# Attention rows of edgeless nodes made beside the gathers of the attention stages, in a fused GNN kernel

## The reference, cut to what matters

```python
def gat_layer(xf, src, dst, W, a_src, a_dst, b, heads, out_ch):
    n = xf.shape[0]
    h = (xf @ W).reshape(n, heads, out_ch)
    e_src = jnp.einsum('nhc,hc->nh', h, a_src)
    e_dst = jnp.einsum('nhc,hc->nh', h, a_dst)
    e = jax.nn.leaky_relu(e_src[src] + e_dst[dst], NEG_SLOPE)
    ...
    out = jax.ops.segment_sum(alpha[:, :, None] * h[src], dst, num_segments=n)
    return out.reshape(n, heads * out_ch) + b
```

## Time and profile before

| | |
|---|---|
| three runs, median (lowest to highest) | 6930.43 us (6916.66 to 6943.3) |
| profiled execution, span | 6960.0 us; no other time of that execution is given |
| TensorE busy | 70% of the span |
| VectorE, ScalarE, GpSimd busy | 55%, 43%, 51% |
| mean granted clock of TensorE | 0.824 |
| plain stage | about 75 to 1963 us |
| stages 8 to 11 | start at about 4717, 5257, 5800 and 6343 us |

### The profile page before, as it was taken

How to read it: one execution, slowest core, us unless ns; L and a number is a source line. 1 busy time by engine, 2 the same in 40 slices (tenths; PEclk the granted TensorE clock), 3 DMA queues, 4 the chain that set the end, 5 groups by cost and what they waited for, 6 DMA issues and landing times. The chain is left out here.

```text
span 6960.0 us, 128354 instructions
## 1 busy us (share of the span) xinstructions
PE 4844.2 (70%) x28287; PEld 3887.0 (56%) x28362; DVE 3822.9 (55%) x13753; ACT 2996.7 (43%) x7457; POOL 3526.6 (51%) x4581
## 2 busy tenths in 40 slices
PE   4888888888889888997798986660381282183087
PEld 3666666666666676666687876650271172073076
DVE  5666666666644586336676767660361261162076
ACT  3666666666633333444566655550130031031043
POOL 2344434444455274706474747106556556656666
PEclk9999999999989856998899987775695596597555
DMA  3555444454444375536633434322232232133233
GB/s 86 150 162 163 166 169 164 162 172 167 166 119 108 110 200 147 144 95 189 194 110 86 115 90 129 87 78 55 54 102 64 48 103 69 42 102 76 46 106 92
DMA packets 1002699, 815.64 MB, mean 117 GB/s; under 512 B 103821, under 2 KB 836819, under 8 KB 1002617
## 3 DMA queue, kind: packets, MB, share of 16 engines
q1 hardware_dynamic: 908536, 650.27, 30.6%
q0 software_dynamic: 94080, 164.48, 9.8%
HBM read 359.28 MB, written 459.01 MB: 118 GB/s over the span
## 5 line engine op out<-in xcount | busy, mean ns | idle before, releaser
L864 POOL DMA_INDIRECT G<-table,idx_all x1568 | 1519.3, 969 | 1308.5 <-issue 661.4
L1436 PE MATMUL PS<-CR,LO 1*128 1x128 f32 (+3 forms) x4312 | 1069.9, 334 | 273.1 <-ACT CR L1763 272.6
L1436 PE MATMUL PS<-G,S 128*128 (+2 forms) x4312 | 995.7, 318 | 41.3 <-DVE OWN L1304 15.6
L1436 PEld LDWEIGHTS PS<-CR,LO 1*128 1x128 f32 (+1 forms) x4312 | 766.1, 221 | 419.7 <-ACT CR L1763 329.8
L1436 PEld LDWEIGHTS PS<-G,S 128*128 128x128 f32 x4312 | 791.2, 223 | 129.8 <-issue 100.5
L1763 ACT ACTIVATE CR<-PS 65x128 f32<-65x128 f32 (+2 forms) x1274 | 340.8, 268 | 1019.0 <-PE PS L1436 1006.7
L864 POOL DMA_INDIRECT G<-table,idx_l x588 | 568.5, 967 | 398.6 <-DMA table<-RO 220.2
L1433 PE MATMUL PS<-ident,ES 128*98 128x128 f32 x16 | 4.2, 420 | 1003.5 <-DVE ES L476 1003.5
L1433 PEld LDWEIGHTS PS<-ident,ES 128*98 128x98 f32 x16 | 2.6, 191 | 1004.7 <-issue 1004.6
L476 DVE COPY ES<-G 128x392 f32<-128x392 f32 x4 | 2.1, 527 | 1017.1 <-DMA G<-table,idx_all 1017.1
L1436 PE MATMUL PS<-G,FS 128*65 (+2 forms) x2646 | 448.5, 314 | 98.8 <-DVE den L1368 44.4
(11 more groups left out here) (291 smaller groups left out, 11312.6 us busy)
## 6 DMA issues: line engine op xcount, KB each, us to landing
table<-G SPq DMA_DIRECT2D x392, 260.0 KB, 2.7
table<-G SPq DMA_DIRECT2D x392, 256.0 KB, 2.6
table<-RO SPq DMA_DIRECT2D x245, 256.0 KB
table<-RO SPq DMA_DIRECT2D x196, 260.0 KB
OWN<-table SPq DMA_DIRECT2D x196, 260.0 KB
XIN<-xrows SPq DMA_DIRECT2D x196, 256.0 KB
OWN<-table SPq DMA_DIRECT2D x147, 256.0 KB
xrows<-RB SPq DMA_DIRECT2D x147, 256.0 KB
```

Source lines behind the costliest of these rows:

```text
L864: g.indirect_dma_start(G[:, t, 0:w], None, TAB[s], bass.IndirectOffsetOnAxis(ap=idx[:, t:t + 1], axis=0)).then_inc(gat[t % 4].sem, 16)
L1436: return nc.tensor.matmul(o, l, r, start=start, stop=stop)
```

## The change

- The plain stage stores one attention table (8) instead of four, and instead of the output it stores the residual rows x3 into a new table `x_plain`. The products, ReLUs, copies and sums of layers 9 to 11 and of the output go from it. All four hand-written orders are new, and the transposes of the edge attributes use another PSUM bank.
- A new function `beside_gathers(s)` runs on SP, TensorE, ScalarE and VectorE at the start of each attention stage, beside GpSimd's gathers. For stages 8, 9 and 10 (kind "F") it goes over all 98 quads: load the rows of table s, four transposes, ReLU with the bias, four products with the next weights, copy, store into table s + 1. For stage 11 (kind "FO") it loads the rows of table 11 and of `x_plain`, adds both and the bias, and stores the output.
- It works in two sets of buffers (b = 0, 1), lent from S and LO, UT and OT, OWN and RO, GN and U.
- GpSimd waits for the stored rows before the next stage's gathers.

```diff
+        F_IN = [t[:, :, :].rearrange("p s c -> p (s c)")[:, 0:4 * GW].rearrange("p (j c) -> p j c", j=4)
+                for t in (S, LO)]
+        F_HT = [UT, OT]
+        F_OUT = [OWN, RO]
+        F_X = [t[:, :].rearrange("p (j c) -> p j c", j=4) for t in (UT, OT)]
+        F_SUM = [GN, U]
...
+        BESIDE = ["F", "F", "F", "FO"]
...
@@ SP @@
             def plain(m, b):
                 q0, q1, q2, q3 = (earlier((m, 0, b), k) for k in range(4))
+                load_x(q0)
+                keep(q1, "t1", q_a[1], "g", PG[1])
+                keep(q3, "x3", q_v[2], "xc", PX[3])
+                keep(q2, "t3", q_a[2], "g", PG[2])
                 keep_x_norm(q3)
-                load_x(q0)
-                keep(q3, "out", q_v[3], "xf", PY)
-                keep(q3, "t3", q_a[2], "g", PG[2])
+                keep_x(q0)
+                next_attributes(q1)
+                keep(q1, "t2", q_a[1], "t1", PR[2])
+                keep(q2, "t4", q_a[2], "rA", PR[4])
+                keep_attributes(q2)
                 keep(q3, "t8", q_v[3], "r8", PR[8])
-                keep_x(q0)
-                keep(q1, "t1", q_a[1], "g", PG[1])
-                keep(q3, "t11", q_v[3], "r11", PR[11])
-                keep(q2, "t4", q_a[2], "rA", PR[4])
-                next_attributes(q1)
-                keep(q3, "t9", q_v[3], "r9", PR[9])
-                keep(q1, "t2", q_a[1], "t1", PR[2])
-                keep(q3, "t10", q_v[3], "r10", PR[10])
-                keep_attributes(q2)
...
+            def beside_gathers(s):
...
+                def load(m, b):
+                    if not isinstance(m, int) or m:
+                        sp.wait_ge(*((f_t.sem, f_t.at(ph, m * 2 + (b - 2), "turn")) if kind == "F" else
+                                     (f_v.sem, f_v.at(ph, m * 2 + (b - 2), "sum"))))
+                    sp.dma_start(F_IN[b], plain_rows(TAB[s], at(m, b) + EP)).then_inc(f_in[b].sem, 16)
+                    if kind == "FO":
+                        sp.dma_start(F_X[b], plain_rows(XP, at(m, b))).then_inc(f_x[b].sem, 16)
+
+                def store(m, b):
...
+                    sp.wait_ge(f_v.sem, f_v.at(ph, m * 2 + b, "rows" if kind == "F" else "sum"))
...
+                def turn(m):
+                    for b in (0, 1):
+                        store(m, b)
+                        if not isinstance(m, int) or m < last:
+                            load(m + 1, b)
+
+                for b in (0, 1):
+                    load(0, b)
+                turn(0)
+                with sp.Fori(1, last - 1) as m:
+                    turn(m)
...
@@ VectorE @@
+                inverse(q3, 3)
+                shift(q3, 3)
                 x_inverse(q1)
                 x_shift(q1)
+                with_bias(q1)
                 stats(q0, 1)
                 aggregate(q0, 1)
+                hidden(q1)
+                inverse(q0, 1)
+                shift(q0, 1)
+                x_stats(q0)
+                convolved(q1)
                 sampled(q2)
+                stats(q1, 2)
                 residual(q2)
+                aggregate(q1, 2)
                 constant(q2)
+                x_aggr(q0)
+                inverse(q1, 2)
+                shift(q1, 2)
                 stats(q2, 3)
                 aggregate(q2, 3)
+                rows(q3, 8)
...
+                def rows(m, b):
+                    dve.wait_ge(f_r.sem, f_r.at(ph, m * 2 + b, "rows"))
+                    free(m, b)
+                    v.tensor_copy(F_OUT[b][:, :, :], pair(2 + 2 * b)).then_inc(f_v.sem, 1)
...
+                def turn(m):
+                    for b in (0, 1):
+                        if kind == "F":
+                            rows(m, b)
+                        else:
+                            bias(m, b)
+                            total(m, b)
...
@@ TensorE @@
+                turned(q1, 1)
+                turned(q2, 2)
                 hidden(q1, 0)
                 hidden(q1, 1)
+                sampled(q2)
+                attributes(q2)
+                convolved(q1)
+                rows_b(q2)
                 rows_a(q2)
+                turned(q3, 3)
+                rows(q3)
...
+                def turned(m, b):
+                    pe.wait_ge(f_in[b].sem, f_in[b].at(ph, m, "rows"))
+                    for j in range(4):
+                        i = turn(PS[:, b, P * j:P * j + P], F_IN[b][:, j, 0:D])
+                    i.then_inc(f_t.sem, 1)
+
+                def rows(m, b):
+                    pe.wait_ge(f_a.sem, f_a.at(ph, m * 2 + b, "hT"))
+                    if not isinstance(m, int) or m:
+                        pe.wait_ge(f_v.sem, f_v.at(ph, m * 2 + (b - 2), "rows"))
+                    rows4(pair(2 + 2 * b), F_HT[b], WX[:, ph + 1, 0:GW]).then_inc(f_r.sem, 1)
+
+                def two(m):
+                    turned(m, 1)
+                    rows(m, 0)
+                    if not isinstance(m, int) or m < last:
+                        turned(m + 1, 0)
+                    rows(m, 1)
+
+                turned(0, 0)
+                two(0)
+                with pe.Fori(1, last) as m:
+                    two(m)
+                two(last)
...
@@ ScalarE @@
+                turned(q1, 1)
+                turned(q2, 2)
+                hidden(q1)
                 sampled(q2)
+                norm(q3, 3)
+                root(q0, 1)
+                x_norm(q1)
                 attributes(q2)
+                convolved(q1)
+                norm(q0, 1)
+                turned(q3, 3)
+                rows_a(q2)
+                root(q1, 2)
+                x_root(q0)
+                norm(q1, 2)
                 root(q2, 3)
...
+                def turned(m, b):
+                    act.wait_ge(f_t.sem, f_t.at(ph, m * 2 + b, "turn"))
+                    f(F_HT[b][:, :], PS[:, b, :], ACT.Relu, bias=gb_c[:, ph:ph + 1]).then_inc(f_a.sem, 1)
```

More of the change, by code:

```diff
@@ L602, in keep @@
                 rows = (rows[q[2]] if isinstance(rows, list) else rows)
-                tab, shift = (out, 0) if name == "out" else (TAB[int(name[1:])], EP)
+                tab, shift = (XP, 0) if name == "x3" else (TAB[int(name[1:])], EP)
                 ready(sp, (done, q, step))
@@ L1138, in rows @@
                 done(q, 3, v.tensor_copy(PR[t], pair(6)))
-            def out_rows(q):
-                if q is None:
-                    return
-                ready(dve, (q_v[3], q, max("r11", "xo", key=q_v[3].order.index)))
-                done(q, 3, v.tensor_tensor(PY, PY, PR[11][:, :, 0:D], ALU.add))
             def x_stats(q):
@@ L1395, in finish_lb, with beside_gathers, free, bias @@
                 coef(s, n, "2")
+            def beside_gathers(s):
+                ph = ATTENTION.index(s)
+                last = PLAIN_TURNS - 1
+                kind = BESIDE[ph]
+                def free(m, b):
+                    if not isinstance(m, int) or m:
+                        dve.wait_ge(f_st[b].sem, f_st[b].at(ph, m))
+                def rows(m, b):
+                    dve.wait_ge(f_r.sem, f_r.at(ph, m * 2 + b, "rows"))
+                    free(m, b)
+                    v.tensor_copy(F_OUT[b][:, :, :], pair(2 + 2 * b)).then_inc(f_v.sem, 1)
+                def bias(m, b):
+                    dve.wait_ge(f_x[b].sem, f_x[b].at(ph, m, "rows"))
+                    v.tensor_tensor(F_X[b], F_X[b], on4(gout_r[:, :]), ALU.add).then_inc(f_v.sem, 1)
+                def total(m, b):
+                    dve.wait_ge(f_in[b].sem, f_in[b].at(ph, m, "rows"))
+                    dve.wait_ge(f_v.sem, f_v.at(ph, m * 2 + b, "bias"))
+                    free(m, b)
+                    v.tensor_tensor(F_SUM[b][:, :, :], F_X[b], F_IN[b][:, :, 0:D], ALU.add).then_inc(f_v.sem, 1)
+                def turn(m):
+                    for b in (0, 1):
+                        if kind == "F":
+                            rows(m, b)
+                        else:
+                            bias(m, b)
+                            total(m, b)
+                turn(0)
+                with dve.Fori(1, last) as m:
+                    turn(m)
+                turn(last)
             for s, kind in STAGES:
@@ L1487, in hidden @@
                 ready(pe, (q_a[1], q, "gT"))
-                before = earlier(q, 1)
-                if half and not q[2] and before is not None:
-                    alone(pe, (e_cp, turn_of(before) + 1))
                 mm(PS[:, 1 + half], w1[:, P * half:P * half + P], PT1[:, :]).then_inc(q_p[1].sem(q), 1)
@@ L2011, in tail_out, with beside_gathers @@
                     attention_rows(s, n, ad_t)
+            def beside_gathers(s):
+                ph = ATTENTION.index(s)
+                last = PLAIN_TURNS - 1
+                if BESIDE[ph] != "F":
+                    return
+                def turned(m, b):
+                    act.wait_ge(f_t.sem, f_t.at(ph, m * 2 + b, "turn"))
+                    f(F_HT[b][:, :], PS[:, b, :], ACT.Relu, bias=gb_c[:, ph:ph + 1]).then_inc(f_a.sem, 1)
+                turned(0, 0)
+                turned(0, 1)
```

(6 more changed lines are left out.)

142 lines of the change are left out of this document (58 added, 84 removed).

## The result

The changed kernel takes **8407.76 us** (median, 8400.13 to 8441.42) where the kernel before took 6926.33 in the same series: ratio **1.2137**, 95% interval 1.2103 to 1.2171, +1481 us. The forecast was 8110, the range 7600 to 8480. The profiled execution spans 8406.5 us, against 6960.0 before.

The account below looks back on a forecast made before the run. The plain stage was taken as bound by a loop through VectorE, SP and a transfer, with idle engines beside the attention stages' gathers. -349 + 1463 + 67 = +1181 on the 6930 us median gave 8110 us, range 7600 to 8480.

Parts of the forecast that it names:

- the whole ring: Stages 8 to 10: store, load, transposes, row products and copy follow one another, 7.45 us per quad, +1463 us in all.
- the third rival: Plain stage: another wait replaces the one removed, the period stays 18.96 us, total 8460 us; chance 0.12.
- The half clock: Stages 8 to 10: TensorE runs at the lower clock level, transposes taking 0.99 and row products 1.73 us.
- the other case: Stages 8 to 10: TensorE keeps 2.4 GHz, 6.25 us per quad, total 7760 us; a rival with chance 0.15.
- The rival of two rings in flight: Stages 8 to 10: one load out per buffer, 7.45 us per pair, total 7017 us; chance 0.06, half of it faster.
- Its point of decision, 3.5 us: Stages 8 to 10: below this time per quad the change was to win.
- rings wholly hidden: Stages 8 to 10: the added work fits entirely behind the gathers, total 6580 us; the faster half of a 0.06 chance.
- part 3: Stage 11: output computed beside the gathers, 6.4 us per pair of quads, +67 us, bounds 0 and +150.
- Part 1: Plain stage: less work per quad shortens the period from 18.96 to 15.4 us, -349 us, between -535 and -143.
- GpSimd isn't in the way: Plain stage: GpSimd's turns take 23.3 and 27.0 us for two quads without the ea_in wait, 13.5 per quad at most.
- The sum of 15.0 + 0.4: Plain stage: a loop from x load through VectorE, TensorE and SP takes 15.0 us, plus 0.4 for slow clock.
- The floor of 5.1 us: Stage 11: a pair's 1.55 MB beside the gathers takes 5.1 us at 371 GB/s.

Follow-up runs that it names:

- e3_load: Changed kernel with SP issuing each next load ahead of the store in stages 8 to 10: ratio 1.0513 to the kernel before.
- e4_order: Changed kernel with TensorE doing the second buffer's row products ahead of the next quad's transposes in stages 8 to 10: ratio 1.1091 to the kernel before.
- e7_two: Changed kernel with the stores of stages 8 to 10 issued by ScalarE, SP issuing only the loads: ratio 1.0134 to the kernel before.
- e5_warm: Changed kernel with five unread 256-column products on TensorE behind each quad's row products in stages 8 to 10: ratio 1.1760 to the kernel before.
- e8_best: Changed kernel with GpSimd's edge-attribute cut behind its node work and stores of stages 8 to 10 on ScalarE's queue: 6716.41 us, ratio 0.9680.
- e1_attr: Changed kernel with the plain stage's edge-attribute transposes one quad earlier on TensorE and ScalarE: ratio 1.1740 to the kernel before.
- e6_noF: Changed kernel without the row computation of stages 8 to 10, SP storing a constant tile instead: ratio 1.0104 to the kernel before.
- e12_fost: e8_best with stage 11's stores moved to ScalarE's queue too: ratio 0.9644 to the kernel before.

## Why the prediction was right, and where it was wrong

**The verdict and its cause: right; the point forecast: 298 us short.** "Every quad goes once round the whole ring, with one load in flight" is what the trace shows, and e3_load, e4_order and e7_two show it by breaking it. The count from the queues' written orders was worth +1463 us and measured +1412. The total is another matter: 8408 us lies next to the 8460 of the third rival, which had a chance of 0.12, and inside the range only because the range was drawn to reach that rival.

**Its terms.** Against 7.45 us the ring took 7.08 behind the gathers, 8.0 beside them, 7.3 in the mean. The load was put at 3.2 for both; it is 2.7 without gathers and 3.4 with them. By the Trainium skill (DMA: Bandwidth & Descriptors, section Anatomy of one DMA), whose fit is for the other issue path, the estimate of the prediction was 2.6 us for 260 KB. The trace agrees within 0.1 behind the gathers (2.7), and not beside them (3.4), a load on the chip for which the formula has no term. The half clock was rightly taken; e5_warm priced the other case at 1.0 us. The rival of two rings in flight had 7.45 us per pair, 3.7 per quad, and a total 1.3% slower than the kernel before, the plain stage's saving included; e3_load has 3.6 and ends 5.1% slower without that saving, an estimated 0.6% with it (1.0513 - 0.0451). By the Trainium skill (Trainium Kernel Development and Optimization, Best Practices), which says to double-buffer, that rival would have been the forecast; the two buffers alone didn't give it. Its point of decision, 3.5 us, is borne out from one side: e7_two has 2.6, and with the plain stage's part (e8_best) the kernel is faster than the one before. The 6580 us that the prediction gives for rings wholly hidden leaves out its own part 3; with those 67 us it is 6650, and e8_best measured 6716.

**Part 1: wrong by its whole size, -349 us forecast, -9 measured.** The step that failed is "GpSimd isn't in the way". It compared GpSimd's own work per turn (23 to 27 us, with its waits left out) with the period of two quads (30.8 us), which is right for an engine that works ahead, and GpSimd would have: e1_attr leaves it 5.2 us of waiting per turn. But its wait for ea_in was left out as if it were slack, without asking what the new orders put in its place. The diff moves TensorE's `attributes` from q1 to q2 and `x_stats` ahead of `convolved`, and the prediction costed both as moves within a sum of durations; the wait `e_tr`, which starts the cut, wasn't followed round. Followed, it reads: transposes, cut, two node gathers, x gathers, x_stats, then the rest of the quad to the next transposes. Its longest stretch, 28.5 us of the 39.06, could be priced before: the gather turn of the earlier trace rows is 27.0. The sum of 15.0 + 0.4 itself came close: with the loop cut, the period is 15.84, 15.65, 15.54 and 15.37 us in four runs. Its terms were not tested one by one, so part of that may be luck. The third rival ("another wait, SP behind x gathers or table 8, takes the place of the one removed") is what happened, and deserved more than its 0.12: SP's wait behind the x gathers is there, beside VectorE's, though what made those gathers late was GpSimd's wait for TensorE, which the rival didn't name.

**Part 3: right in sign, mis-sized.** +67 forecast, +87 measured. One pair of stage 11, VectorE and SP (timeline), and the time of x_plain's loads from issue to landing there:

```profile
7801.27 0.69 DVE L1467 TENSOR_TENSOR OT<-OT,gout_r 128x512 f32<-128x512 f32 x1 [2.14 <-DMA OT<-x_plain]
...
7801.99 0.69 DVE L1473 TENSOR_TENSOR U<-OT,LO 128x512 f32<-128x512 f32 x1
...
7802.87 0.36 SPq L710 DMA_DIRECT2D out_x<-U  x1
...
7804.03 0.33 SPq L701 DMA_DIRECT2D OT<-x_plain  x1
...
7808.50 0.69 DVE L1467 TENSOR_TENSOR OT<-OT,gout_r 128x512 f32<-128x512 f32 x1 [2.30 <-DMA OT<-x_plain]
```

```profile
DMA to landing us min/median/max: 3.8/4.1/4.7
```

From 7801.27 to 7808.50 are 7.2 us for this pair (6.8 in the mean) where 6.4 was taken. The term is the load, 3.4 in the forecast and 4.1 here. The floor of 5.1 us by the bandwidth of one slice of 2 us was never reached.

**The sum.** -349 + 1463 + 67 = +1181 against -9 + 1412 + 87 = +1490 on the traces, less 44 us in code that the change leaves alone: +1446. The error on the spans, +265 us, is part 1 (+340), the ring (-51), part 3 (+20) and that code (-44); the ring's error and the unchanged code hid 95 us of part 1's error, which is luck. The medians lie 1481 us apart, 35 more than the two spans.

## What to carry to other kernels

Two buffers are two loads in flight only if no in-order queue has the load behind something that depends on the other buffer: write out each queue's order and walk one turn round, as was done here for SP and TensorE, before counting on overlap; where the store waits for the end of the chain, taking it off the loads' queue was worth 1387 us here. Walk the same way round every wait that an edit moves, also for an engine that has time to spare: GpSimd with 25 us of work in 31 set the pace of the plain stage because its turn began with a wait for TensorE and ended with what VectorE stood waiting for. And work moved into idle time is worth what one pass of its ring costs against the cover per pass (here 7.3 us against 2.5), not what its instructions sum to.

## What the hardware did that had not been expected

- Loads of 256 to 260 KB landed after 2.7 us with little else under way, 3.4 beside gathers at 122 GB/s and 4.1 at 272 GB/s. The prediction took 3.2 us for the first two, and 3.4 where the third stood.
- Adding products whose result nobody reads to a ring that waits for DMA made it 14% shorter (7.3 to 6.3 us). The granted clock of the stretches is 0.55, most of it at the lower level of 1.2 GHz, where TensorE did 2.9 us of work and then waited 4.1 us or more per quad; 0.91 with the added products and waits of 2.0 us; and 0.99, 2.4 GHz nearly throughout, in e7_two, with waits of 1.0 us in the mean and 1.9 at most.
- 98 stores of 260 KB issued back to back beside the gathers (e6_noF, 188 us of SP's time) added 5 us to the phase, though the DMA share stood at 1.05, higher than the 0.92 of e12_fost at 293 GB/s. So a share near 1 doesn't say by itself that the bandwidth is used up:

```profile
4700.00:4900.00 200.00, 0.00 (x0) 0.00 (x0) 0.00 (x0) 0.00 (x0) 147.63 (x157) 0.50 1.05 172
```
